# Pooled attention's exponentials in one slot, the choice of experts in other slots, and one operand read with a stride

## The reference

```python
qkv = x @ Wqkv.T + bqkv                       # 8 heads of 16
lm_idx = jnp.arange(0, N, N // 16)[:16]
q_lm, k_lm = q[:, :, lm_idx], k[:, :, lm_idx]
kernel_1 = softmax(q    @ k_lm.T * scale)     # 1024 x 16
kernel_2 = softmax(q_lm @ k_lm.T * scale)     # 16 x 16
kernel_3 = softmax(q_lm @ k.T    * scale)     # 16 x 1024
z = kernel_2.T / sum(kernel_2 ** 2)
for _ in range(6):
    z = 2.0 * z - z @ kernel_2 @ z
t = t + (kernel_1 @ (z @ (kernel_3 @ v))) @ Wproj.T + bproj
xt = layernorm(t)
gate = softmax(xt @ Wg); topv, topi = top_k(gate, 2)       # choice of experts
t = t + sum over the 2 chosen e of score * (gelu(xt @ W1[e] + b1[e]) @ W2[e] + b2[e])
```

## Time and profile before

| | |
|---|---|
| median of 3 runs | 5571.4 us (5562.84 to 5574.16) |
| profiled execution, span | 5548.6 us; its own whole time isn't listed |
| PE busy | 4842.2 us (87%) |
| DVE busy | 3586.2 us (65%) |
| ACT busy | 2987.7 us (54%) |
| POOL busy | 1021.9 us (18%) |
| mean granted TensorE clock | 0.952 |

### The profile page before, as it was taken

One profiled execution on the slowest core, in us unless ns is written; L12 is line 12 of the kernel. 1 busy time (PEld: TensorE's weight loads), 2 busy tenths in 40 slices (PEclk: granted clock), 3 DMA queues, 4 the chain that ended last, 5 costly groups with the idle time before them and its releaser, 6 DMA issues.

```text
span 5548.6 us, 81822 instructions
## 1 busy us (share of the span) xinstructions
PE 4842.2 (87%) x25633; PEld 2616.5 (47%) x25633; DVE 3586.2 (65%) x7699; ACT 2987.7 (54%) x5420; POOL 1021.9 (18%) x1348
## 2 busy tenths in 40 slices
PE   5888888888888886957888888888899999999999
PEld 1222222222222221336777877787755555555554
DVE  6677777777777762555665656555576676766765
ACT  2655565665655653414555555556755455455552
POOL 2212112121222112202333333333210000000000
PEclk7999999999999998979999999999999999999999
DMA  2522222222222211223545454544321111111112
GB/s 84 144 70 81 81 70 70 70 73 78 73 89 82 66 45 38 29 68 106 165 140 163 141 162 147 157 146 129 106 61 45 50 48 45 50 46 47 52 45 75
DMA packets 406297, 477.10 MB, mean 86 GB/s; under 512 B 87640, under 2 KB 249648, under 8 KB 403760
## 3 DMA queue, kind: packets, MB, share of 16 engines
q1 hardware_dynamic: 372128, 424.84, 25.4%
q0 software_dynamic: 20576, 35.55, 2.3%
q10 hardware_dynamic: 13168, 11.48, 0.8%
HBM read 308.54 MB, written 145.57 MB: 82 GB/s over the span
## 4 chain that ended last, share of the span: by engine, by line
PE 33%; DVE 15%; issue 3%; DVEq 3%; ACT 2%; ACTq 0%; SPq 0%; DMA 0%
PE n_ps_f L2153 4%; PE n_ps_f L2146 4%; PE n_ps_xy L1801 3%; PE n_ps_h L1791 3%; PE n_ps_c L2193 2%; PE n_ps_h L2205 2%; PE n_ps_f L2140 2%; PE n_ps_f L1649 2%; PE n_ps_xy L2209 1%; DVEq L2025 1%; DVE n_stats L971 1%; DVE n_xln L983 1%; PE n_ps_f L995 1%; PE n_ps_h L2209 1%; DVE n_down_weights L2024 1%
## 5 line engine op out<-in xcount | busy, mean ns | idle before, releaser
L597 ACT ACTIVATE a_probs<-ps_b 128x512 f32<-128x512 f32 x2048 | 1111.0, 594 | 794.8 <-PE ps_b L693 782.0
L454 DVE TENSOR_REDUCE a_negmax<-ps_a 128x1 f32<-128x1024 f32 x1024 | 1206.1, 1219 | 378.9 <-PE ps_a L637 369.3
L637 PE MATMUL ps_a<-a_k_stack,a_q_stack 96*128 96x512 bf16 x2048 | 634.6, 396 | 178.8 <-DVE a_negmax L454 89.9
L693 PE MATMUL ps_b<-a_q_stack,a_k_stack 99*128 99x512 bf16 x2048 | 673.6, 391 | 68.2 <-ACT a_probs L597 30.9
L1604 ACT ACTIVATE n_hidden<-n_ps_h,n_b 128x128 f32<-128x128 f32 x1472 | 420.2, 374 | 339.1 <-PE n_ps_h L1791 338.3
L706 PE MATMUL ps_o<-a_probs,a_v_ones 128*32 128x512 f32 x4096 | 562.0, 622 | 0.2 <-ACT a_probs L597 0.2
L637 PEld LDWEIGHTS ps_a<-a_k_stack,a_q_stack 96*128 96x128 bf16 x2048 | 146.1, 99 | 732.2 <-DVE a_negmax L454 468.9
L1801 PE MATMUL n_ps_xy<-n_down_weights,n_hidden 128*128 x2944 | 410.7, 284 | 78.9 <-ACT n_xy L1618 72.8
L693 PEld LDWEIGHTS ps_b<-a_q_stack,a_k_stack 99*128 99x128 bf16 x2048 | 196.2, 100 | 487.8 <-ACT a_probs L597 251.5
L1801 PEld LDWEIGHTS n_ps_xy<-n_down_weights,n_hidden 128*128 128x128 f32 x2944 | 369.1, 196 | 117.0 <-issue 112.8
L1791 PE MATMUL n_ps_h<-n_xy,n_up_weights 128*128 128x128 f32 x2944 | 399.8, 279 | 3.6 <-issue 1.8
(11 more groups left out here) (346 smaller groups left out, 7532.8 us busy)
## 6 DMA issues: line engine op xcount, KB each, us to landing
n_up_weights<-in_L_ffn_W_dram SPq DMA_DIRECT2D x368, 256.0 KB, 2.7
n_up_weights<-score_scratch SPq DMA_DIRECT2D x512, 128.0 KB, 2.9
split_scratch<-a_pieces SPq DMA_DIRECT2D x180, 256.0 KB
a_q_stack<-split_scratch SPq DMA_DIRECT2D x128, 192.0 KB, 3.7
a_k_stack<-split_scratch SPq DMA_DIRECT2D x128, 192.0 KB, 4.1
rows_scratch<-n_zero SPq DMA_DIRECT2D x16, 1472.0 KB, 10.5
outs_scratch<-n_xy SPq DMA_DIRECT2D x176, 128.0 KB, 1.9
n_xg<-rows_scratch SPq DMA_DIRECT2D x80, 256.0 KB
```

Of the source, the lines that this page charges most:

```text
L454: dve.tensor_reduce(negmax[:, b, t:t + 1], bank, axis=AX.X, op=ALU.max, negate=True).then_inc(ring_read, 1)
L597: act.activation(probs[:, m % PROBS, 512 * k:512 * k + 512], ps_b[:, k, :], ACT.Exp).then_inc(b_exp, 1)
L637: last = pe.matmul(bank[:, cols], q_stack[0:KS, h, 128 * t:128 * t + 128], k_stack[0:KS, h, cols], start=True, stop=True)
L693: pe.matmul(ps_b[:, k, :], k_stack[:, h, 128 * t:128 * t + 128], q_stack[:, h, 512 * k:512 * k + 512], start=True, stop=True).then_inc(b_u ...
```

## The change

The constant `NEWTON_AT` = 25 is the slot of Newton step 0 (24 before). On PE `front` runs S1 (slot 18) and S3 (slot 19, in `pa`) ahead of v (slot 21, after k1's subtraction), and the landmark product for S2 is gone: DVE reads S2 as every 64th column of S3. DVE subtracts S1's maxima in slot 19, does S2 and S3's maximum in slot 20 and v in slot 22. ACT does all three exponentials in slot 21; kernel 3 is written over `qt` instead of `xt`. The norm of the inverse (slot 24) also waits for kernel 3's exponential, because it writes into `pa`. Kernel 1's sums follow Newton step 0, its scaling step 1. Later steps stand one slot later.

`choice`: the norm's statistics stay in slot 0, its square root and scaling go to slot 4, in buffers of their own; all other pieces move by 2 to 4 slots, as the diff shows.

```diff
+        NEWTON_AT = 25
-        e3 = sb("xt", [128, NT, 128])
-        xt, qt, kt = e3[:, :, :].rearrange("p t n -> p (t n)"), sb("qt", [128, N]), sb("kt", [128, N])
+        xt, qt, kt = sb("xt", [128, N]), sb("qt", [128, N]), sb("kt", [128, N])
+        e3 = qt[:, :].rearrange("p (t n) -> p t n", t=NT)
...
                 last.then_inc(S["lm_up"], 1)
-                yield 18
+                yield 19
+
+                s1 = pb_[:, :].rearrange("p (g l) -> p g l", l=LM)
+                k1v = k1[:, :, :].rearrange("p t (h l) -> p (t h) l", l=LM)
+                dve.wait_ge(S["s1_ps"], i + 1)
+                dve.tensor_reduce(max1[:, :], s1, axis=AX.X, op=ALU.max)
+                dve.drain()
+                dve.tensor_tensor(k1v, s1, max1[:, :].unsqueeze(2).broadcast_to((128, NT * HEADS, LM)), ALU.subtract).then_inc(S["k1_sub"], 1)
+                yield 20
+
+                s2 = pa[:, 0:N:STEP]
+                dve.wait_ge(S["s3_ps"], i + 1)
+                dve.tensor_reduce(max2[:, :], s2, axis=AX.X, op=ALU.max)
+                dve.drain()
+                dve.tensor_scalar(e2[:, :], s2, max2[:, :], None, ALU.subtract).then_inc(S["e2_sub"], 1)
+                dve.tensor_reduce(max3[:, :], pa[:, :], axis=AX.X, op=ALU.max)
+                dve.drain()
+                dve.tensor_scalar(max3[:, :], max3[:, :], -SCALE, None, ALU.mult).then_inc(S["max3_up"], 1)
+                yield 22
                 dve.wait_ge(S["v_ps"], i + 1)
...
-                yield 22
-                dve.wait_ge(S["e_up"], i * 2 + 1)
+                yield 23
+                dve.wait_ge(S["e2_up"], i + 1)
...
-                    if it == 1:
-
-                        dve.wait_ge(S["s3_ps"], i + 1)
-                        dve.tensor_reduce(max3[:, :], pb_[:, :], axis=AX.X, op=ALU.max)
-                        dve.drain()
-                        dve.tensor_scalar(max3[:, :], max3[:, :], -SCALE, None, ALU.mult).then_inc(S["max3_up"], 1)
-                    if it == 2:
-                        dve.wait_ge(S["e_up"], i * 2 + 2)
+                    if it == 0:
+                        dve.wait_ge(S["k1_exp"], i + 1)
                         dve.tensor_reduce(sum1[:, :], k1v, axis=AX.X, op=ALU.add)
                         dve.drain()
                         dve.reciprocal(sum1[:, :], sum1[:, :])
                         dve.drain()
+                    if it == 1:
                         dve.tensor_tensor(k1v, k1v, sum1[:, :].unsqueeze(2).broadcast_to((128, NT * HEADS, LM)), ALU.mult).then_inc(S["k1_up"], 1)
...
-                token_norm(dve, xln2, tok, stats, mv, var, inv, tmp).then_inc(S["ln2_up"], 1)
-                yield 10
+                for n, last in enumerate(token_norm_steps(dve, xln2, tok, stats2, mv2, var2, inv2, tmp2)):
+                    if n == 2:
+                        yield 4
+                last.then_inc(S["ln2_up"], 1)
+                yield 12
...
-                    yield 32 + 2 * k
+                    yield 36 + 2 * k
                     dve.wait_ge(S["b2_ps"], i * HALVES + k + 1)
...
                 yield 21
-                act.wait_ge(S["d_up"], i * 2 + 1)
-                act.activation(e2[:, :], e2[:, :], ACT.Exp, scale=SCALE, accum_out=sum2[:, :]).then_inc(S["e_up"], 1)
-                act.wait_ge(S["d_up"], i * 2 + 2)
-                act.activation(k1[:, :, :], k1[:, :, :], ACT.Exp, scale=SCALE).then_inc(S["e_up"], 1)
-                yield 28
+                act.wait_ge(S["k1_sub"], i + 1)
+                act.activation(k1[:, :, :], k1[:, :, :], ACT.Exp, scale=SCALE).then_inc(S["k1_exp"], 1)
+                act.wait_ge(S["e2_sub"], i + 1)
+                act.activation(e2[:, :], e2[:, :], ACT.Exp, scale=SCALE, accum_out=sum2[:, :]).then_inc(S["e2_up"], 1)
                 act.wait_ge(S["max3_up"], i + 1)
-                act.activation(e3[:, :, :].rearrange("p t n -> p (t n)"), pb_[:, :], ACT.Exp, scale=SCALE, bias=max3[:, :], accum_out=sum3[:, :]).then_inc(S["e3_up"], 1)
+                act.activation(qt[:, :], pa[:, :], ACT.Exp, scale=SCALE, bias=max3[:, :], accum_out=sum3[:, :]).then_inc(S["e3_up"], 1)
...
-                yield 11
+                yield 14
                 act.wait_ge(S["shift_up"], i + 1)
...
+                yield 18
+                pe.wait_ge(S["lm_up"], i + 1)
+                for t in range(NT):
+                    last = pe.matmul(pb_[:, 128 * t:128 * t + 128], qt[:, 128 * t:128 * t + 128], k_lm[:, :], start=True, stop=True)
+                last.then_inc(S["s1_ps"], 1)
+                yield 19
+                wide(pa, q_lm[:, :], kt).then_inc(S["s3_ps"], 1)
+                yield 21
+                pe.wait_ge(S["k1_sub"], i + 1)
                 for t in range(NT):
                     last = pe.matmul(pb_[:, 128 * t:128 * t + 128], xt[:, 128 * t:128 * t + 128], wqkv[:, 2 * C:3 * C], start=True, stop=True)
                 last.then_inc(S["v_ps"], 1)
-                yield 19
-                pe.wait_ge(S["lm_up"], i + 1)
-                pe.matmul(pa[:, 0:LM], q_lm[:, :], kt[:, 0:N:STEP], start=True, stop=True).then_inc(S["s_ps"], 1)
...
+                yield NEWTON_AT - 1
+
+                pe.wait_ge(S["e3_up"], i + 1)
                 pe.wait_ge(S["m2_up"], i + 1)
...
-                    if it == 0:
-                        pe.wait_ge(S["d_up"], i * 2 + 2)
-                        wide(pb_, q_lm[:, :], kt).then_inc(S["s3_ps"], 1)
                     if it == 3:
-                        pe.wait_ge(S["e3_up"], i + 1)
+                        pe.wait_ge(S["v_up"], i + 1)
                         pe.wait_ge(S["k1_up"], i + 1)
...
-                yield 22
+                yield 26
                 pe.wait_ge(S["score_up"], i + 1)
...
-                    yield 31 + 2 * k
+                    yield 34 + 2 * k
```

More of the change, by code:

```diff
@@ L1108, in landmark_and_gelu_phase @@
         gate = gate_tiles(sb, E)
+        spare = gate["above"][:, :, :].rearrange("p a f -> p (a f)")
+        stats2, mv2 = spare[:, 0:6 * NT].rearrange("p (t s) -> p t s", t=NT), spare[:, 6 * NT:8 * NT].rearrange("p (t s) -> p t s", t=NT)
+        var2, inv2, tmp2 = (spare[:, n * NT:(n + 1) * NT] for n in (8, 9, 10))
         score_t = sb("score_t", [2 * E, N])
@@ L1137, in landmark_and_gelu_phase @@
         COUNTED = NT * E + E
-        events = ("x1_in y_in y_turned gate_ps x2_up tok_ps tok_up ln_up lnt_ps xt_up qk_ps v_ps qk_up v_up lm_up s_ps s3_ps "
-                  "d_up e_up m2_up norm_ps fro_in z0_up k1_up turned_ps turned_up max3_up e3_up kv_ps kv_up mixed_ps mixed_up attn_ps attn_up "
+        events = ("x1_in y_in y_turned gate_ps x2_up tok_ps tok_up ln_up lnt_ps xt_up qk_ps v_ps qk_up v_up lm_up s1_ps s3_ps "
+                  "k1_sub e2_sub e2_up k1_exp m2_up norm_ps fro_in z0_up k1_up turned_ps turned_up max3_up e3_up kv_ps kv_up mixed_ps mixed_up attn_ps attn_up "
                   "ln2_up lnt2_ps xt2_up router_ps shift_up exp_up score_up scores_ps st_up b2_ps base_up count_ps count_read routed owner_up")
@@ L1386, in front @@
                 for it in range(NEWTON):
-                    yield 24 + 2 * it
+                    yield NEWTON_AT + 2 * it
                     dve.drain()
@@ L1494, in choice @@
                 gate_shift(dve, gate, E).then_inc(S["shift_up"], 1)
-                yield 13
+                yield 16
                 dve.wait_ge(S["exp_up"], i + 1)
-                yield from spread(13, gate_choose_steps(dve, gate, E, K, 1e-6, tie[:, :]))
+                yield from spread(16, gate_choose_steps(dve, gate, E, K, 1e-6, tie[:, :]))
                 dve.drain()
-                yield from spread(21, running_sums(), 0)
+                yield from spread(24, running_sums(), 0)
                 dve.drain().then_inc(S["score_up"], 1)
-                yield 23
+                yield 27
                 dve.wait_ge(S["count_ps"], i + 1)
@@ L1589, in choice @@
                 for k in range(HALVES):
-                    yield 25 + 2 * k
+                    yield 29 + 2 * k
                     act.wait_ge(S["scores_ps"], i * HALVES + k + 1)
@@ L1673, in front @@
                 last.then_inc(S["v_ps"], 1)
-                yield 19
-                pe.wait_ge(S["lm_up"], i + 1)
-                pe.matmul(pa[:, 0:LM], q_lm[:, :], kt[:, 0:N:STEP], start=True, stop=True).then_inc(S["s_ps"], 1)
-                yield 20
-                pe.wait_ge(S["v_up"], i + 1)
-                for t in range(NT):
-                    last = pe.matmul(pb_[:, 128 * t:128 * t + 128], qt[:, 128 * t:128 * t + 128], k_lm[:, :], start=True, stop=True)
-                last.then_inc(S["s_ps"], 1)
-                yield 23
+                yield NEWTON_AT - 1
+                pe.wait_ge(S["e3_up"], i + 1)
                 pe.wait_ge(S["m2_up"], i + 1)
@@ L1713, in front @@
                 last.then_inc(S["kv_ps"], 1)
-                yield 38
+                yield NEWTON_AT + 14
                 pe.wait_ge(z_up, i * NEWTON + NEWTON)
@@ L1729, in choice @@
                 for k in range(HALVES):
```

(4 more changed lines are left out.)

41 lines of the change are left out of this document (13 added, 28 removed).

## The result

| | before | changed |
|---|---|---|
| median, first measurement | 5567.1 us (4 runs) | 5489.4 us (5477.9 to 5492.9, 4 runs) |
| changed / before | | 0.9858, 95% interval 0.9844 to 0.9873 |
| the same pair again (after_again) | 5556.7 us (9 runs) | 5494.5 us (5486.3 to 5495.4, 4 runs) |
| changed / before | | 0.9888, 95% interval 0.9873 to 0.9903 |
| span of the profiled execution | 5548.6 us | 5476.1 us |

The changed kernel is faster by 62 to 78 us, where 37 us were forecast. Its median lies inside the range of 5484 to 5576; the size is what was wrong: 1.7 to 2.1 times the forecast saving.

A forecast was written before the change was run, and what follows sets the result against it. PE, busy 79.8 of a 90.7 us cycle, bounds the kernel, with 10.9 us of waiting. Savings of 27 (waits), 7 (clock) and 3 us (first images) make -37: from 5571.4 to 5534 us, range 5484 to 5576.

The forecast's parts named there:

- Part 1: Norm split, slots 0 and 4: slot 6's 2.05 us wait goes, 1.2 us (0 to 2) comes at slot 8.
- Part 2: Router's exponential from slot 11 to 14: slot 15's 2.1 us wait goes, 0.8 us (0 to 1.7) at slot 18.
- Part 3: All exponentials in slot 21: slot 31's 1.18 us wait goes, 2.4 us (1.3 to 4) at slots 24 and 25.
- Part 4: Order around S1, S3 and v: Newton waits of 1.6 us (1 to 3) against 2.1; slot 22's 1.3 us goes.
- Part 5: Second b2 product moved to PE slot 36: new wait of 1.3 us (0.8 to 2).
- Part 6: Scatter rows four slots later, 25.8 us left for a 26.0 us chain: 0.2 us wait (0 to 2).
- The sum: Listed waits per cycle 10.15 to 8.7 us; with S2's product and gap ends 1.95 us less, 27 over fourteen cycles.
- the clock: PE's half-speed time costs 1.6 us a cycle beyond the cleanest; 0.5 of it comes back, 7 us in all.
- The first two images: Run without experts; lose a wide product and a maximum from the Newton chain, gain 1.9 us ahead: -3 us.
- B: Rival: new waits at slots 8, 18, 36 mostly hidden, full 1.6 us of clock recovered; 5484 us; chance 0.14.
- C: Rival: slower by the scatter, routing one Newton step (3.8 us) late, PE waits at slot 45; 5587 us; chance 0.08.
- the other signs: Four table loads an image instead of six; no PE wait at L1659, L1746; one pair-copy wait; listed new waits.

The follow-up runs named there:

- after_again: The changed kernel itself run again beside other kernels on one chip: 5494.5 us, 0.9888 of the kernel before.
- e5: The changed kernel with one unused 128 x 1 exponential in slot 28, so two table loads return there: 5494.7 us, 0.9887 of before.
- e1: The kernel before with only `choice` changed; attention's exponentials stay in slots 21 and 28: 5517.9 us, 0.9930 of before.
- e6: The changed kernel with the second b2 product on PE in slot 37 instead of 36: 5490.0 us, 0.9879 of before.
- e3: The kernel before with unused spare matmuls, 8 ahead of the wait at slot 6 and 9 ahead of slot 15's: 5546.3 us, 0.9969 of before.
- e4b: The changed kernel with 5, 8 and 5 unused spare matmuls at slots 8, 24 and 36, a repetition: 5465.1 us, 0.9839 of before.
- e7: The changed kernel with the choice's norm whole in slot 0 again: 5529.3 us, 0.9944 of before.
- e8: The changed kernel with the norm whole in slot 0 and the router's turn, logits and exponential back in slots 6 to 11: 5566.8 us, 1.0008 of before.
- e2: The changed kernel with `choice` as in the kernel before: 5514.7 us, 0.9923 of before.

## Why the prediction was wrong in size

**The bound.** Right: PE's waits set the cycle, and all of the gain lies in the landmark stage.

**Part 1** (norm in two parts). Right in mechanism and size: 1.2 us forecast at slot 8, 15.8 / 13 = 1.2 measured; the wait at slot 6 is gone.

**Part 2** (router's exponential). Right: slot 15 is free of waits, 0.8 us forecast at slot 18, 0.7 measured.

**Part 3** (exponentials). 2.4 us forecast at slots 24 and 25, 2.0 + 0.1 measured. The value of the loads was put as part of a block whose wait goes; e5 agrees, since the loads alone bring no wait back. That the wait of slot 31 needs this part of the change is not shown: it goes in e1 without it.

**Part 4.** Newton's waits were mis-sized: 1.6 us forecast, 12.6 / 14 + 2.5 / 14 = 1.1 measured. The strided read costs 0.16 to 0.17 us for the maximum and 0.23 us for the subtraction in the changed kernel's trace, and the 16 dense columns of before cost the same: no difference, as forecast.

**Part 5.** 1.3 us forecast, 1.36 measured.

**Part 6.** 0.2 us forecast, 0.2 measured in the first profile (2.3 us in 5 waits over 14 cycles) and 0.4 in after_again. That nothing is left there was right too, and e6 shows it; but the prediction didn't say that it caps any further saving ahead of slot 45.

**The sum.** This is the step that failed, in three of its terms. Us a cycle:

| | forecast | first profile | after_again |
|---|---|---|---|
| PE's listed waits | -1.45 | -2.8 | -2.5 |
| the clock | -0.5 | -1.45 | -0.8 |
| the rest: S2's product 0.14, ends of gaps 0.35 | -0.5 | -1.1 | -1.25 |
| cycle | -2.45 | -5.3 | -4.6 |

Of the 2.1 to 2.9 us that the sum missed, 1.1 to 1.3 are waits, 0.3 to 0.95 the clock and 0.65 to 0.75 the rest.

*Waits.* The new ones were all at their forecast places. After the change the named ones add up to 7.7 us where the sum had 8.7: Newton's are 0.5 smaller, those of slots 24 and 25 0.3, the others 0.2. Another 0.35 are small waits that the sum left out.

*Clock.* The prediction counted the loss beyond the cleanest cycle, 1.6 us, as the whole loss, and gave back 0.5 of it. But no cycle of before was free of it; the cleanest had a granted clock of 0.98 and a low stretch of its own. The whole loss was some 3.15 us. It was also spread over the cycle as if it were a background, where it hangs on certain waits, and the change took away those of slots 6, 15, 31 and 33. e3, e4b and e7 show it for slots 6, 15, 25 and 36; for slots 31 and 33 it is read from the traces alone. How much came back is less firm: there is one trace of before, and three of the changed schedule (e5 taken in) have 3.4, 4.7 and 5.3 us of low clock, so the gain lies between 0.5 and 1.45 us. At its lower end the forecast of 0.5 was right.

*The rest.* PE's busy time, less half the low clock, is 76.7 us a cycle before and 75.5 and 75.4 in the two profiles of the changed kernel. The sum took every step as 0.89 us, the distance of two neighbours on a PE that doesn't wait, and changed only the number of waits. In the traces an up step, up to the next instruction or the wait ahead of it and outside the low stretches, takes 0.96 us on average before and 0.94 after, a down step 0.94 and 0.93: 0.022 and 0.011 us a step, with 23 of each about 0.75 us a cycle, and S2's product another 0.14. The longest of them, up to 1.15 us, stand ahead of waits, so a wait costs a little more than its entry in the list. What makes up the remaining 0.2 to 0.4 us stays open, and no run tests this part.

With Newton at 1.1, slots 24 and 25 at 2.1 and the clock at 1.45, the prediction's sum would have given 4.2 us a cycle, 59 us for the fourteen.

**The first two images** were to give 3 us: 154.1 us from the first turn to the third before, 152.9 and 154.1 after. Between nothing and 1 us.

**Rivals.** B (new waits mostly hidden, clock recovered) had the time, 5484, and half of the reason: the new waits are all there, 1.2, 0.7 and 1.36 us where it had 0, 0 and 0.8, but the clock gave back 0.8 to 1.45 of its 1.6 us. The time lies inside the stated range only because the range took in B, which is no merit of the sum. The cycle of 88 us among the signs was wrong, 85.4 to 86.1; the other signs came. C is real as a mechanism, at 1.6 to 1.9 us a cycle in e1 and e6, well below its price of 3.8; in the changed kernel it takes 0.2 to 0.4 us.

## What to carry to other kernels

When an engine's clock depends on what it did before, a wait has two prices, its own length and the clock lost behind it: list the low stretches with the waits ahead of them before summing, and count against full clock, not against the cleanest piece. The loss varies from one execution to the next, so take it from more than one trace. Look in an in-order kernel for what a late instruction holds: putting the residual ahead of half a norm (two lines and buffers of its own) was worth 3.2 us of 85 with the rest of the change in place, while two table loads less were worth nothing measurable. Undo a part together with what was moved for its sake: e8 keeps the late slots without the exponential that needed them, and lies 47 us behind e2. When a wait is removed, the next chain that ends there (here sixteen scatters, a load and a turn) decides how much of it is kept.

## What was not expected of the hardware

Work whose result nobody reads made the kernel faster: with 18 spare matmuls a cycle in PE's waits the time fell from 5494.5 to 5465.1 us, and the time at the lower of the two clock levels (1.2 GHz against 2.4) from 4.7 to 1.05 us a cycle. The Trainium skill ("TensorE: Matmul & The Clock Gate", The HAM clock gate) describes an array that goes to half clock when it has been idle. The traces agree: all low stretches of the thirteen cycles before and after stand at or right behind a wait of PE, and 13 of the 20 before are gone in e3, where two of these waits are filled. At slot 36 the clock fell behind a wait of 1.36 us with shorter ones near it.
